# Selective scan on one core: how TensorE orders the two spreads of a half tile and their waits

## What is computed

```python
u_c = silu(conv(u))                                    # 512 channels
dt  = softplus(dt_r @ W_dt.T + b_dt)                   # step sizes
def step(h, inp):                                      # 16 states a channel
    dA = exp(dt_t[..., None] * A)
    h  = dA * h + (dt_t * u_t)[..., None] * B_t[:, None, :]
    y_t = einsum('bds,bs->bd', h, C_t)
```

## Time and profile before

| what | value |
|---|---|
| three executions | 4112.15, 4117.29, 4157.99 us |
| time of the profiled execution | 4109.0 us |
| its span | 4107.2 us |
| mean granted PE clock over the span | 0.874 |
| PE busy | 3116.8 us (76%) |
| PE weight loads (PEld) busy | 2436.5 us (59%) |
| DVE busy | 1891.7 us (46%) |
| ACT busy | 1386.5 us (34%) |
| POOL busy | 916.0 us (22%) |

### The profile page before, as it was taken

The page is one execution under the profiler, slowest core; times in us unless marked ns, Lnnn a source line. Parts: engine busy times, 40 slices in busy tenths (PEclk is TensorE's granted clock), DMA queues, the critical chain, the costliest instruction groups (busy, mean ns, idle before and its releaser), DMA issues. The chain is left out here.

```text
span 4107.2 us, 76937 instructions
## 1 busy us (share of the span) xinstructions
PE 3116.8 (76%) x27490; PEld 2436.5 (59%) x27552; DVE 1891.7 (46%) x3976; ACT 1386.5 (34%) x3684; POOL 916.0 (22%) x1207
## 2 busy tenths in 40 slices
PE   5888863236769988939938688888886959788777
PEld 5777752114556656726626576767664647566666
DVE  4889873353436655621147523333331236533321
ACT  3556531102325545513316422222221325422211
POOL 2666652321111122140042200101011022201000
PEclk9999985557989999959969899899996989889989
DMA  3000000000000000041120100000005110100000
GB/s 112 2 3 2 2 15 28 21 0 22 0 22 14 13 14 4 1 170 45 44 60 0 63 15 5 8 5 5 5 0 210 34 44 1 39 13 15 22 7 20
DMA packets 80798, 113.81 MB, mean 28 GB/s; under 512 B 11600, under 2 KB 59600, under 8 KB 79712
## 3 DMA queue, kind: packets, MB, share of 16 engines
q1 hardware_dynamic: 70992, 93.43, 6.8%
q0 software_dynamic: 4608, 12.59, 0.9%
q10 hardware_dynamic: 5008, 5.11, 0.4%
HBM read 89.48 MB, written 21.63 MB: 27 GB/s over the span
## 5 line engine op out<-in xcount | busy, mean ns | idle before, releaser
L2904 POOL TENSOR_TENSOR hc<-h,bc 128x1024 f32<-128x1024 f32 x128 | 301.9, 2359 | 177.7 <-DVE h L3171 163.9
L3171 DVE TENSOR_TENSOR_SCAN h<-da,dbu_ps 128x1024 f32<-128x1024 f32 x128 | 292.3, 2283 | 10.4 <-DVE dbu_ps L3183 4.8
L1349 ACT ACTIVATE probs<-s_ps,negmax 128x128 f32<-128x128 f32 (+1 forms) x768 | 239.7, 425 | 7.0 <-DVE negmax L1412 6.4
L696 ACT ACTIVATE probs<-s_ps,negmax 128x128 f32<-128x128 f32 x384 | 130.8, 366 | 304.3 <-DVE negmax L744 293.0
L1223 PE MATMUL t_ps<-ident,probs 128*128 128x128 f32 x1280 | 204.9, 283 | 35.5 <-DVE pT L1419 32.6
L335 POOL TENSOR_TENSOR var_eps<-mv,ln_eps 128x1 f32<-128x1 f32 x96 | 18.3, 190 | 868.9 <-DVE mv L321 868.9
L1223 PEld LDWEIGHTS t_ps<-ident,probs 128*128 128x128 f32 x1280 | 139.9, 141 | 96.6 <-issue 62.1
L2989 PE MATMUL dta_ps<-dt,a_spread 32*128 32x128 f32 x2048 | 158.5, 296 | 47.2 <-ACT da L3117 25.7
L3183 DVE TENSOR_TENSOR dbu_ps<-dbu_ps,bc 128x1024 f32<-128x1024 f32 x128 | 155.6, 1216 | 63.4 <-PE dbu_ps L2994 63.2
L1357 ACT ACTIVATE pT<-t_ps 128x512 f32<-128x512 f32 x160 | 95.7, 598 | 251.5 <-PE t_ps L1223 251.3
L3117 ACT ACTIVATE da<-dta_ps 128x1016 f32<-128x1016 f32 x128 | 130.3, 1018 | 139.0 <-PE dta_ps L2989 138.6
(11 more groups left out here) (415 smaller groups left out, 7545.0 us busy)
## 6 DMA issues: line engine op xcount, KB each, us to landing
c_in<-in_ctx SPq DMA_DIRECT2D x64, 256.0 KB, 2.6
w_up<-in_L_ffn_w SPq DMA_DIRECT2D x8, 1024.0 KB, 13.3
w_down<-in_L_ffn_w SPq DMA_DIRECT2D x8, 1024.0 KB, 12.1
rows<-expert_rows_in SPq DMA_DIRECT2D x62, 128.0 KB, 2.1
expert_rows_out<-y SPq DMA_DIRECT2D x62, 128.0 KB, 1.7
expert_rows_in<-zeros ACTq DMA_DIRECT2D x1, 4992.0 KB, 28.5
w_gate<-in_L_ffn_w SPq DMA_DIRECT2D x8, 512.0 KB, 9.6
w_up<-in_L_ffn_w SPq DMA_DIRECT2D x8, 512.0 KB, 9.5
```

What stands on the lines that cost most here:

```text
L1349: last = act.activation(probs[:, u % 2, i, k, :], src, ACT.Exp, bias=negmax[:, u % 2, HB * i + k:HB * i + k + 1])
L2904: pool.tensor_tensor(hc[:, s % 4], h[:, s % 2], bc[:, j, 1, :].unsqueeze(1).broadcast_to([P, 2 * G, P]), ALU.mult).then_inc(hc_ready.sem, 1)
L3171: dve.tensor_tensor_scan(flat(h[:, s % 2]), flat(da[:, s % 4]), dbu_ps[s % 2][:, :, :, :].rearrange("p i g t -> p (i g t)"), 0.0, ALU.mult ...
```

## The change

`spread_out` is rewritten. It now issues first the wait and the eight matmuls of the inputs (half tile s + 1), and after them the wait and the eight matmuls of the steps (half tile s + 2). The rows, the weights, the buffers and the number of matmuls stay the same, and so does every wait, but `da_ready` and `dt_ready` now stand behind the matmuls of the inputs. Matmuls of the one kind no longer alternate with those of the other, so that at a time only two of the four strips are addressed.

```diff
                 def spread_out(steps, inputs):
+                    if inputs is not None:
+                        b, j, s = inputs
+                        if s == 0:
+                            pe.wait_ge(dtu_ready.sem, dtu_ready.done(b))
+                        pe.wait_ge(scanned.sem, scanned.done(H * b + s - 2))
+                        for g in range(G):
+                            for i in range(2):
+                                row = ROWS * (2 * (s % 2) + i)
+                                last = pe.matmul(dbu_ps[s % 2][:, i, g, :], spread_sb[row:row + ROWS, g, :],
+                                                 dtu[row:row + ROWS, j, s // 2, :], start=True, stop=True)
+                        last.then_inc(dtu_made.sem, 1)
                     if steps is not None:
                         b, j, s = steps
                         if s == 0:
                             pe.wait_ge(dt_ready.sem, dt_ready.done(b))
                         pe.wait_ge(da_ready.sem, da_ready.done(H * b + s - 1))
-                    if inputs is not None:
-                        bi, ji, si = inputs
-                        if si == 0:
-                            pe.wait_ge(dtu_ready.sem, dtu_ready.done(bi))
-                        pe.wait_ge(scanned.sem, scanned.done(H * bi + si - 2))
-                    for g in range(G):
-                        for i in range(2):
-                            if steps is not None:
+                        for g in range(G):
+                            for i in range(2):
                                 row = ROWS * (2 * (s % 2) + i)
-                                last_a = pe.matmul(dta_ps[:, i, g, :], a_spread[row:row + ROWS, s // 2, g, :],
-                                                   dt[row:row + ROWS, j, s // 2, :], start=True, stop=True)
-                        for i in range(2):
-                            if inputs is not None:
-                                row = ROWS * (2 * (si % 2) + i)
-                                last_u = pe.matmul(dbu_ps[si % 2][:, i, g, :], spread_sb[row:row + ROWS, g, :],
-                                                   dtu[row:row + ROWS, ji, si // 2, :], start=True, stop=True)
-                        if g == G - 1:
-                            if steps is not None:
-                                last_a.then_inc(dta_made.sem, 1)
-                            if inputs is not None:
-                                last_u.then_inc(dtu_made.sem, 1)
+                                last = pe.matmul(dta_ps[:, i, g, :], a_spread[row:row + ROWS, s // 2, g, :],
+                                                 dt[row:row + ROWS, j, s // 2, :], start=True, stop=True)
+                        last.then_inc(dta_made.sem, 1)
```

## The result

The changed kernel takes 4150.75 us (median of 20 executions, 4142.81 to 4161.59), the kernel before 4116.93 us. The ratio is 1.008, with a 95% interval from 1.0065 to 1.0094: 34 us more. Forecast were 4170 us, in a range from 4122 to 4220.

What follows compares the result with a forecast made beforehand. DVE was taken to bound the kernel before, PE after the change. Full-clock terms of +64 us and -5 for the clock gave +59 on 4109.0, so 4168 us, forecast as 4170, range 4122 to 4220.

Steps and rivals of the forecast that it cites:

- What bounds the kernel: Between the scans DVE sets the pace, with PE only 2 us behind it in a sequence.
- Two strips cost as many rounds as four: In `spread_out`, a spread of one kind takes eight rounds, 0.97 us of loads, despite half the matmuls.
- 0.88 us for the second eight rounds, at least 0.77: PE time the steps' block adds behind the inputs in each spread; 7.0 us a sequence.
- PE's remaining waits: PE idle kept per sequence: 0.37 us for decay, 0.34 ahead of `project_xd`, 1.1 ahead of `project_u`; together 1.8 us.
- The clock: Half-clock stretches between the scans, priced at 15.9 us before, might vanish or grow by 4 or 24; taken as -5 us.
- The sum: +64 us at full clock less 5 for clock changes: +59 on the profiled execution's 4109.0, giving 4168 us.
- the last sequence, put at 0: Sequence 15, at the end of the stage, was expected to add 0 us.
- the first rival: In a spread, steps' rounds run beside the inputs', so PE's work does not grow; 4069 or rather 4085 us, chance 0.07.
- The second rival: The steps' block adds only 0.5 to 0.7 us, or PE's clock stays full, or both; 4130 to 4150 us, chance 0.21.
- the forecast's own 4150 to 4200: Range in us for the main case, PE becoming the bound through added spread work; chance 0.60.
- its own list: Signs of a wrong prediction: two kinds' rounds overlap, a two-strip round under 0.11 us, clock moving over 0.05, other stages moving.

Runs made afterwards that it cites:

- One strip at a time: Changed kernel with PE's loop written out, each block issuing all matmuls of one strip before those of the other; 4323.95 us, ratio 1.0491.
- staggered: PE's loop written out, each kind with its own wait, half the inputs ahead of the steps' wait, then both alternating; 4098.45 us, ratio 0.995 to the kernel before.
- the first mixed kernel: Kernel before, with inputs ahead of steps, each with its own wait, only in iterations 0 and 2; 4147.14 us, ratio 1.0067.
- Two strips: Changed kernel with PE's program written out instead of its hardware loop; 4130.47 us, ratio 1.0029 to the kernel before.

## Why the prediction was right in kind and too high

- **What bounds the kernel.** Right. PE stood 2 us behind DVE in a sequence, and the change put it ahead.
- **Two strips cost as many rounds as four.** Right: rounds are 0.11 us apart in both. The 3.07x of the Trainium skill (TensorE: Matmul & The Clock Gate, Part 3) was measured with 512 columns, here there are 128, and it isn't what makes the second block cheaper. What does agrees with the Trainium skill, same page, Part 2, by which loads for other row groups are pulled ahead: the trace after shows the steps' loads 0.56 us behind the first of the inputs, up to three rounds before the inputs end. That page also keeps the matmuls themselves in program order; the records here do not show that order (383.78 for a matmul of the steps, 384.11 for one of the inputs ahead of it).
- **0.88 us for the second eight rounds, at least 0.77.** This step failed. It measured 0.55 to 0.56, below the lower bound, because the two blocks overlap. I had taken it from `step_sizes`, which starts one round behind a spread (345.13, 345.25), and called that a block on a strip of its own. It contracts rows 0 to 15 and thus lies in the first strip, which the spread itself uses, so it could not start sooner. A block on free strips had no row before. One strip at a time (2.75 us) and staggered (1.21 us) confirm the three rounds a strip, give or take one. The term was worth 8 x 0.33 = 2.6 us of PE's work a sequence, 37 us in 14.
- **PE's remaining waits.** 1.8 us forecast; in the changed kernel the decay wait is 0.50 us (0.37 forecast), the one ahead of `project_u` 1.49 (1.1). The decay wait belongs to iterations 1 and 3, which I had called 0 and 2; the sum did not depend on it, the first mixed kernel did. Ahead of `project_xd` PE waits 0.55 us (0.34). These waits grow when the spread gets shorter: the one ahead of `project_u` is 3.1 us less the spread, so 1.1 with 1.98 and 1.45 with 1.65. So the sequence doesn't fall by the whole 2.6 us. With the measured spread and these waits the sum is 27.5 + 4.4 + 0.50 + 0.55 + 1.49 = 34.4 us, and 34.27 came: 2.0 below the forecast of 36.3, 28 us in 14 sequences.
- **The clock.** I took -5 us. It was 0.95 in the loop sequences before and is 0.96 after, so most of its price stayed. The argument behind it, that a PE rarely idle keeps its clock, doesn't hold in general: one strip at a time was busy 46.36 of 46.99 us at 0.85.
- **The sum.** +59 us forecast; +45.8 in the profiled execution, +34 in the medians. With the 28 us off it would have been +31, and the profiled executions differ by 39.8 between the scans and by 6.0 outside them. So the forecast was too high by one term and too low by others, and part of its nearness is luck. Of the others one shows: the last sequence, put at 0, grew from 27.94 to 31.46 us at clocks of 0.74 and 0.66. In the chances I gave 0.26 to a change within 1%, and it is that.
- **The rivals.** The blocks do overlap, as the first rival had it, by three rounds of 16; not under the 0.3 us a spread that it needed to make the kernel faster. The second rival, *half hidden*, is what happened: its condition was 0.5 to 0.7 us a spread (0.56 came), its time 4130 to 4150 us (4150.75 came). That the time also lies at the lower edge of the forecast's own 4150 to 4200 says nothing for the forecast's mechanism. By its own list the prediction named overlapping rounds as a sign that it is wrong, and rounds of the two kinds do overlap.

## What to carry to other kernels

Matmuls that contract 32 rows are worth issuing so that all four strips have work at once; but they needn't alternate strictly, since in these traces each strip took about three rounds in advance. To price a block that follows another, find a row where the two really use different strips. And before giving PE more work to fill a wait, compare its own work with the period: here 2 us of slack stood against 4.4 us of added work, and the filled wait was none that DVE felt.

## What the runs showed that was not expected

- A busy PE does not by itself keep the full clock. One strip at a time: busy 46.36 of 46.99 us, clock 0.85. Two strips: 32.37 of 34.15 us, clock 1.00.
- Small edits move the clock by more than their own cost. Putting two waits together cost some 0.5 us a sequence as work and 1.7 to 3.4 us through a clock of 0.95 and 0.91. Why the clock fell there stays open.
- The head of PE's hardware loop costs 1.8 us of idle PE each time. Written out, the kernel before gains 25 to 29 us for six heads. In the profiles 18 of them lie between the scans: 11 are that idle, and some 7 fit less half clock (0.94 to 0.96). The others lie behind the last scan, where the code is the same.
